# A two-layer block on one core: the far queries' maxima move to VectorE, the biases move into the last channel, start-up and weight loading are rearranged

## The reference, cut to what matters

```python
xn = _layernorm(x, axis=-1)
Q = (xn @ Wq + bq).reshape(b, s, H, C) * inv_sqrt_c       # H, C = 16, 64
K = (xn @ Wk + bk).reshape(b, s, H, C)
V = (xn @ Wv + bv).reshape(b, s, H, C)
scores = jnp.einsum('bshq,bshk->bshqk', Q, K)             # per token and head: 64 x 64
scores = jnp.where(triu(ones((C, C)), 1), -inf, scores)
attn = jnp.einsum('bshqk,bshk->bshq', softmax(scores), V)
x = x + attn @ Wo + bo + (silu(xn @ wg.T) * (xn @ wu.T)) @ wd.T
```

## Time and profile before

| | us |
|---|---|
| runs (3) | 3949.12, 3951.41, 3953.07 |
| the profiled execution | 3948.97 |
| its span, first to last instruction | 3947.2 |
| PE, DVE, POOL, ACT busy in the span | 3548.3, 3260.5, 3342.6, 1973.2 |
| 500 to 830: experts | 330 |
| 834 to 957: combine | 123 |
| 961 to 3947: last stage | 2986 |

### The profile page before, as it was taken

The page is one execution under the profiler, slowest core; times in us unless marked ns, Lnnn a source line. Parts: engine busy times, 40 slices in busy tenths (PEclk is TensorE's granted clock), DMA queues, the critical chain, the costliest instruction groups (busy, mean ns, idle before and its releaser), DMA issues.

```text
span 3947.2 us, 72250 instructions
## 1 busy us (share of the span) xinstructions
PE 3548.3 (90%) x25960; PEld 3110.3 (79%) x26155; DVE 3260.5 (83%) x3712; ACT 1973.2 (50%) x2535; POOL 3342.6 (85%) x1498
## 2 busy tenths in 40 slices
PE   5594999966899999999999999999999999999999
PEld 4253888854688888888888888888888888888888
DVE  8332666647798899999999999899999999999988
ACT  1010333334555555555555655565555566555555
POOL 1675665622899999999999999999999999999997
PEclk8797999987999999999999999999999999999999
DMA  9323565676000000000000000000000000000000
GB/s 380 125 104 123 172 184 178 188 266 236 3 5 5 5 5 5 5 5 5 5 6 6 8 5 5 5 5 5 5 5 6 5 7 5 6 7 5 5 5 5
DMA packets 110635, 209.30 MB, mean 53 GB/s; under 512 B 16610, under 2 KB 77282, under 8 KB 110306
## 3 DMA queue, kind: packets, MB, share of 16 engines
q1 hardware_dynamic: 84192, 140.90, 11.2%
q0 software_dynamic: 21504, 59.93, 4.0%
q10 hardware_dynamic: 4608, 4.20, 0.3%
...
## 4 chain that ended last, share of the span: by engine, by line
POOL 37%; PE 18%; issue 15%; DVE 3%; ACT 1%; another core or an unknown queue 0%; POOLq 0%; DVEq 0%; ACTq 0%
POOL at_s L1276 34%; PE at_num L1509 7%; PE at_den L1509 6%; PE at_work L1487 3%; POOL at_m L1261 1%; POOL at_fall L1258 1%; PE at_work L1497 1%; DVE at_pv L1195 1%; DVE at_k_low L1422 1%; PE at_misc L1541 1%; PE at_misc L1535 1%; ACT at_s L1355 1%; DVE at_s L1195 1%; POOL at_m L1256 0%; DVE at_k_top L1419 0%
## 5 line engine op out<-in xcount | busy, mean ns | idle before, releaser
L1276 POOL TENSOR_TENSOR at_s<-at_s,at_m 128x2048 f32<-128x2048 f32 (+7 forms) x768 | 2511.1, 3305 | 32.6 <-DVE at_s L1195 24.5
L1355 ACT ACTIVATE at_s<-at_s 128x2048 f32<-128x2048 f32 (+7 forms) x768 | 1080.5, 1418 | 610.2 <-POOL at_s L1276 609.9
L1509 PE MATMUL at_den<-k_ident,at_s 128*128 128x128 f32 x9216 | 1135.2, 273 | 53.3 <-ACT at_s L1355 53.2
L1509 PE MATMUL at_num<-k_ident,at_pv 128*128 128x128 f32 x9216 | 1141.7, 274 | 15.8 <-issue 5.6
L1509 PEld LDWEIGHTS at_num<-k_ident,at_pv 128*128 128x128 f32 x9216 | 1048.0, 142 | 92.1 <-issue 70.3
L1509 PEld LDWEIGHTS at_den<-k_ident,at_s 128*128 128x128 f32 x9216 | 1037.0, 141 | 85.0 <-ACT at_s L1355 61.0
L1196 DVE TENSOR_TENSOR at_pv<-at_s,at_vp 128x2048 f32<-128x2048 f32 (+7 forms) x512 | 688.7, 1345 | 226.2 <-ACT at_vp L1330 179.9
L1196 DVE TENSOR_TENSOR at_s<-at_q,at_kp 128x2048 f32<-128x2048 f32 (+7 forms) x512 | 687.9, 1344 | 13.7 <-ACT at_kp L1325 10.0
L1195 DVE TENSOR_TENSOR at_pv<-at_s,at_vp 128x2048 f32<-128x2048 f32 x256 | 582.7, 2276 | 0.0
L1195 DVE TENSOR_TENSOR at_s<-at_q,at_kp 128x2048 f32<-128x2048 f32 x256 | 580.1, 2266 | 0.0
L1487 PE MATMUL at_work<-k_region,at_xT 128*128 128x512 f32 x788 | 406.0, 641 | 105.9 <-ACT at_k_far L1296 82.2
(11 more groups left out here) (232 smaller groups left out, 3396.6 us busy)
## 6 DMA issues: line engine op xcount, KB each, us to landing
moe_w<-experts SPq DMA_DIRECT2D x256, 384.0 KB
...
moe_x<-slot_x SPq DMA_DIRECT2D x256, 134.0 KB, 2.3
...
picked<-moe_yo,moe_row POOLq DMA_INDIRECT x256, 3.1
...
```

Of the source, the lines that this page charges most:

```text
L1276: nc.gpsimd.tensor_tensor(part(s_slot, c), part(s_slot, c), by_query(m[unit_of(c)][:], c), ALU.subtract).then_inc(sub_done, 1)
L1355: nc.scalar.activation(part(s_slot, c), part(s_slot, c), ACT.Exp, scale=C ** -0.5).then_inc(exp_done, 1)
L1509: ins = nc.tensor.matmul(dst[:, b * P:(b + 1) * P], buf[:, at:at + P], k.ident[:], start=(c in (0, NTRI) and x == 0 and b == 0), stop=Fals ...
```

## The change

Five things. (1) The far maxima's three operations go from POOL (chunks 2 to 4) to VectorE: two products after `products` of chunk 3, the difference after `products` of chunk 4. The near ones stay on POOL. ScalarE's copy of V's far half for the next products is asked for one chunk earlier (`SHOW_V` 17 to 16). (2) There is no bias matmul: the last channel of the normalised input is set to 1, the last row of each weight is subtracted from the other rows (a normalised row sums to zero), and the bias is written in the last row's place; the up weights get the same subtraction. (3) Only the leading cells of each row of `s_slot` and `pv_slot` are cleared, inside the main block. (4) K0, K1, Q0 and V0 of tile 0 go to four banks (`work`, `misc`, `num[1]`, `den[1]`), so none waits for another. (5) Wq, Wk, Wv and Wo are loaded during the experts, after turns 6, 12, 18 and 24, by SP.

```diff
@@ routed_experts, SP
                 for i in range(TURNS):
                     turn_in(i)
+                    if i in (6, 12, 18, 24):
+                        dst, name = late[i // 6 - 1]
+                        sp.dma_start(dst[:], io[name].rearrange("(c p) n -> p c n", p=P)).then_inc(late_in, 16)
+                sp.wait_ge(late_in, 16 * len(late))
@@ combine, VectorE
                     if step == 0:
-                        dve.wait_ge(w_in, 160)
+                        dve.wait_ge(w_in, W_ALL)
                         c.mark(v.memset(k.keep_max[:], 0.0))
                         c.mark(v.memset(k.keep_min[:], 0.0))
-                        c.mark(v.memset(k.part_rows[:], 0.0))
-                        c.mark(v.tensor_copy(parts, rest[:]))
...
-                        c.mark(v.tensor_tensor(rest[:], rest[:], parts, ALU.subtract))
-                    elif step == 2:
-                        c(v.tensor_copy(parts[64:128, :], rest[64:128, :]))
-                    elif step == 3:
-                        c(v.tensor_tensor(rest[64:128, :], rest[64:128, :], parts[64:128, :], ALU.subtract))
-                    elif step == 4:
-                        c(v.tensor_copy(parts[96:128, :], rest[96:128, :]))
+                    if step < 3:
+                        w = k.wqkv[step]
+                        v.tensor_tensor(w[:], w[:], view(last[:], [[0, DC], [1, HC]], step * HC), ALU.subtract
+                                        ).then_inc(shifted, 1)
+                    elif step < 5:
+                        s = stage[step - 3][:].rearrange("p (c n) -> p c n", c=DC)
+                        c(v.tensor_tensor(s, s, view(last_up[:], [[0, DC], [1, HID]], (step - 3) * HID), ALU.subtract))
@@ combine, SP
-                for i, name in enumerate(("WqT", "WkT", "WvT")):
-                    sp.dma_start(k.wqkv[i][:], io[name].rearrange("(c p) n -> p c n", p=P)).then_inc(w_in, 16)
-                for i, name in enumerate(("bq", "bk", "bv")):
-                    sp.dma_start(rest[:, i * HC:(i + 1) * HC], io[name].partition_broadcast(P)).then_inc(w_in, 16)
-                sp.dma_start(k.wo[:], io["Wo"].rearrange("(c p) n -> p c n", p=P)).then_inc(w_in, 16)
+                    sp.dma_start(last[:, i, :], io[name][D - 1].partition_broadcast(P)).then_inc(w_in, 16)
+                for i, name in enumerate(("wgT", "wuT")):
+                    sp.dma_start(last_up[:, i, :], io[name][D - 1].partition_broadcast(P)).then_inc(w_in, 16)
...
+                sp.wait_ge(shifted, 3)
+                for i, name in enumerate(("bq", "bk", "bv")):
+                    sp.dma_start(k.wqkv[i][P - 1:P, DC - 1, :], io[name].rearrange("(o n) -> o n", o=1)).then_inc(bias_in, 16)
@@ attention_and_ffn
+        def lead(ring, i):
+            return view(ring[i][:], [[WIDTH[i % 2], ROWS], [1, PREFIX[i % 2]]])
...
-            @block.vector
-            def _(dve):
-                for t in s_slot:
-                    nc.vector.memset(t[:], 0.0).then_inc(zeroed, 1)
-                dve.wait_ge(zeroed, S_RING)
@@ ScalarE
+                    if h:
+                        act.wait_ge(max_near, t * 3 + 3)
+                    else:
+                        wait(act, max_far, t * 3)
+                    nc.scalar.activation(fall[:], bank[:], ACT.Relu, scale=-1.0).then_inc(q_out, 1)
...
-                SHOW_V, SHOW_K_FAR, SHOW_K_NEXT = {1: 0, 17: 1}, 13, 21
+                SHOW_V, SHOW_K_FAR, SHOW_K_NEXT = {1: 0, 16: 1}, 13, 21
@@ VectorE
+                def far_maxima(t, step):
+                    if step == 0:
+                        dve.wait_ge(q_out, t * 2 + 2)
+                        v.tensor_tensor(by_row(m[1]), by_head(k_top, 1), by_row(m[1]), ALU.mult).then_inc(max_far, 1)
+                        v.tensor_tensor(by_row(fall), by_head(k_low, 1), by_row(fall), ALU.mult).then_inc(max_far, 1)
+                    else:
+                        dve.wait_ge(max_far, t * 3 + 2)
+                        v.tensor_tensor(m[1][:, 0:HALF], m[1][:, 0:HALF], fall[:], ALU.subtract).then_inc(max_far, 1)
...
                         products(t, c)
+                        if c in FAR_MAXIMA:                       # {3: 0, 4: 1}
+                            far_maxima(t, FAR_MAXIMA[c])
@@ TensorE
-                        nc.tensor.matmul(work[:], xT[u][:, c, :], wqkv[which][:, c, cols], start=(c == 0), stop=False)
-                    nc.tensor.matmul(work[:], part_rows[:], bias[:, which, cols], start=False, stop=True
-                                     ).then_inc(work_done, 1)
+                        ins = nc.tensor.matmul(bank[:], xT[u][:, c, :], wqkv[which][:, c, cols], start=(c == 0),
+                                               stop=(c == DC - 1))
+                    ins.then_inc(work_done, 1)
```

More of the change, by code:

```diff
@@ L901, in combine @@
         stage = [a.sb(f"stage{i}", [P, DC * HID], I32) for i in range(3)]
-        rest = a.sb("rest", [P, 3 * HC])
+        last = a.sb("last", [P, 3, HC])
+        last_up = a.sb("last_up", [P, 2, HID], I32)
+        shifted, bias_in, ones_set = a.sem("shifted"), a.sem("bias_in"), a.sem("ones_set")
         tr = [a.ps(f"tr{j}", [P, DC, P]) for j in range(2)]
@@ L1194, in multiply @@
             if is_rect(c):
[L1195 removed]
+                return nc.vector.tensor_tensor(in_rows(out), in_rows(other), keys, ALU.mult)
             return nc.vector.tensor_tensor(out, other, keys, ALU.mult)
[L1198 to L1212 removed]
+        def lead(ring, i):
+            return view(ring[i][:], [[WIDTH[i % 2], ROWS], [1, PREFIX[i % 2]]])
         with nc.Block() as block:
@@ L1410, in times_v, with scan @@
                     multiply(part(pv_slot, c), part(s_slot, c), by_key(vp[:], c), c).then_inc(pv_done, 1)
-                def scan(t, half, step, use):
+                def scan(t, half, step, use, bank=work):
                     flat = lambda x: x[:].rearrange("p h c -> p (h c)")
@@ L1468, in tile @@
                             output(t - 1)
+                for i in range(S_RING):
+                    v.memset(lead(s_slot, i), 0.0).then_inc(zeroed, 1)
                 for half in range(2):
                     for step in range(2):
-                        scan(0, half, step, half + 1)
+                        scan(0, half, step, half + 1, (work, misc)[half])
+                dve.wait_ge(zeroed, S_RING)
+                dve.wait_ge(padded, 4 + PV_RING)
                 tile_loop(dve, tile)
@@ L1481, in _, with project @@
             def _(pe):
-                def project(t, u, which, half):
+                def project(t, u, which, half, bank=work):
                     pe.wait_ge(xT_in[u], 8 * (t - u) + 16)
```

112 lines of the change are left out of this document (55 added, 57 removed).

## The result

The changed kernel takes 3973.28 us (median of four, 3970.88 to 3977.87), the kernel before 3951.64 on the same chip: a ratio of 1.0057, 95% interval 1.0039 to 1.0074. It is slower by 0.4 to 0.7%. The forecast was 3975, slower, and held. The profiled execution took 3970.88, its span is 3969.1, 21.9 us over the span before.

The account below looks back on a forecast made before the run. It took a 90.14 us tile loop through PE, ScalarE and DVE, not POOL, as the bound. Start -25, combine -9.5, experts +10 and tiles +50 gave +25.5 over 3948.97, 3974.5; it said 3975 us, range 3928 to 3995.

Parts of the forecast that it names:

- loop of waits: Last stage's tile: a loop through PE, ScalarE and DVE of 90.14 us, mean 91.38, with POOL in none of its links.
- The hold: DVE's two far products in the tile wait for POOL's chunk 3 subtraction: pair 1.85 us late, +2.45 with the difference; 0.50.
- The bias: Four bias matmuls in PE's link of the tile, 0.86 us: removing them gains nothing, the time goes into waiting.
- long ones: Tiles where PE leaves its 2.4 us wait slow: 92.4 or 94.7 us, against 92.6 for a short tile.
- Start of the stage: Start of the last stage: earlier tile data saves 15 us, projections without waits about 10; -25 us (-20 to -28).
- Combine: Combine: 8.8 us less wait for the sixth tile of rows, 1 or 2 less DVE work; -9.5 us (-6 to -12).
- Experts: Experts: SP's four 1 MB loads stand ahead of rows; +10 us, between nothing and four times 3.5.
- The sign that I had named: Experts: PE's stall behind SP's loads; forecast wrong if it is absent or much above 3 us each.
- Nothing is held: Rival: DVE's far operations in the tile are not held by POOL; +0.25 us a tile, 3935 us; chance 0.29.
- Held only to the end of the subtraction in hand: Rival: DVE's pair starts right after POOL's current subtraction; +0.8 us a tile, 3951 us, no change; chance 0.13.
- The third also held: Rival: DVE's third far operation loses to POOL's subtraction too; +2.4 us a tile more, 4050 us; chance 0.04.
- POOL is the bound: Rival: POOL, 97% busy, limits the last stage; tile falls by about 3 us, 3835 us; chance 0.04.

Follow-up runs that it names:

- runs 1: The changed kernel with the three far maxima back on POOL at chunks 2, 3 and 4: 3871.4 us, ratio 0.9802 to the kernel before.
- run 3: The changed kernel with DVE's two far products reading q from its PSUM bank, not relu(q) from SBUF: 3909.2 us, ratio 0.9898 to the kernel before.
- run 4: The changed kernel with one more wait, POOL starting chunk 3's subtraction only after DVE's two far products: 3938.0 us, ratio 0.9975 to the kernel before.
- run 5: The kernel before without the bias matmul of each projection, biases left out of the computation: 3891.3 us, ratio 0.9859 to the kernel before.
- run 8: The changed kernel with far maxima on POOL and ScalarE's first copy of V ahead of the copies of q: 3828.2 us, ratio 0.97 to the kernel before.
- run 2: The kernel before with only the far maxima moved to DVE, after the products of chunks 3 and 4: 4010.8 us, ratio 1.0155 to the kernel before.
- run 11: The changed kernel with a fifth matmul, of zeros, in every projection in the bias matmul's place: 3988.6 us, ratio 1.0113 to the kernel before.
- run 7: The changed kernel with ScalarE's second copy of V back at chunk 17 in place of 16: 3964.0 us, ratio 1.0041 to the kernel before.
- run 9: The changed kernel with the four 1 MB weights fetched in the combine again, not in the experts: 3973.9 us, ratio 1.0076 to the kernel before.

## Why the prediction was right, point by point

**The bound.** The loop of waits was right for the kernel before, and so was the link at its top, DVE's first product with V. From `fall` to that product it takes 0.88, 2.02, 2.27 and 3.96 us on the mean in runs 1, 3, 4 and the changed kernel, and the tile takes 90.11, 91.41, 92.14 and 93.30: 3.1 us more there, 3.2 more in the tile. That POOL was no bound at 97% is shown by 5, where PE's four short matmuls alone took 1.6 us off the tile, and by 8, where POOL gets to 99.6%. "POOL is in none of its links" stopped being true with the change: there it is POOL's subtraction of chunk 0, and no longer PE's Q1, that lets ScalarE go on to `fall`.

**The hold.** Right in kind, and too small: 3.98 us instead of 2.73. Two sizes were off. The product's own length was taken as 0.69 from a row whose operands lie in sequence; with POOL at rest it is 1.02 (run 4). `k_top` is read by head, 256 bytes apart, in a pattern of 32 by 16, and that is what I see as different, since the difference of the third operation, with both operands in SBUF and in sequence, takes 0.68; the stride wasn't tried by itself. The trace of before had the hint: POOL's same product takes 1.55. And DVE was held twice, because `fall` comes out while POOL is still in chunk 2. I had left `fall` at its old place against POOL, 0.4 us behind chunk 2, although 0.86 us of PE's work ahead of it were gone. In run 2, with PE's bias matmuls in place, it came while POOL was in chunk 3, DVE was held once, and it took 2.98 in the median: 1.23 of waiting for POOL where I had 1.44, and 1.75 for the pair where I had 1.29. In run 11 both kinds of tile occur.

**The bias.** I put the 0.86 at nothing, lost to waiting. That is most of it: in run 11 the pair takes up 0.79. But the tile gave 0.59 of it back. In the kernel before it was worth 1.6 (run 5), since fewer tiles were long. Added to the far maxima alone, +2.05 (run 2), and `SHOW_V`, +0.27 (run 7, put at 0): less the 0.59, the parts give +1.73, of 1.92 measured. My +1.6 was near it because I had priced the far maxima about right (+2.45 in a short tile, less on the mean, against 2.05 alone and 3.19 last), not because the parts add up: what each is worth depends on which others are there. There is luck in it too. I had 92.6 for a short tile and came to 93.0 by adding long ones; measured were 93.3 in nearly every tile, and hardly a longer one to add.

**Once only.** Start of the stage: from clearing to tile 0's product 121.7 before and 97.65 after, -24.1; forecast -25. Combine: from its first issue to the clearing 961.61 - 834.39 = 127.2 before and 950.69 - 837.01 = 113.7 after, -13.5; forecast -9.5. DVE's wait for the sixth tile fell as the bytes say, 20.35 to 11.73, 8.6. What I mis-sized is the rest of the stage, 1 to 2 us put down to DVE's operations where 4.9 came off (and 8.8 with 1 or 2 is 10 to 11, not the 9.5 that I wrote). In run 9, where DVE's work is that of the changed kernel, 13.9 - 11.7 = 2.2 us of its difference also lie behind that wait, so about half of the 4.9 belongs to the loads. Experts: +2.6 in the two profiles, about +6 over fourteen; forecast +10, inside its bounds. The sign that I had named is there, but small: 8 to 10 us behind each of the four loads PE waits for its rows in the changed kernel, 2.58, 1.48, 1.67 and 0.92 us, 6.6 together, where in run 9 the waits at these places are 0.3 to 0.7.

**The total.** 3973 against 3975 is closer than the terms are. The tiles cost 59.5 us and not 50; start, combine and experts gave 35.0 together and not 24.5, and 2.6 more came off behind the last tile. The two misses, 9.5 one way and 13.1 the other, cancel by luck.

**The rivals.** "Nothing is held" falls with run 3: it would have been the faster side, and it is what a kernel gets whose operand is in PSUM. "Held only to the end of the subtraction in hand" falls with the changed kernel's own rows and run 4: POOL's next subtraction gets its turn between the two products. "The third also held" doesn't occur; it is POOL that waits there, 0.37 us. "POOL is the bound" was wrong for this kernel and is right for run 8.
